# Output row pairs on partitions 0 to 99 for one quad of batches and on 28 to 127 for the next

## The chip, the cores and the metric

The kernel runs on one core of a Trainium2 chip. The metric is the device time of one execution in microseconds; before the change the median of three runs is 1459.87 us (1458.11, 1459.87 and 1463.94).

## What is computed

For 2048 batches of 200 fields with 64 features each, every field is multiplied by a 64 x 64 weight of its own, and the results are multiplied with all fields of the same batch. All values are fp32; the output is 2048 x 200 x 200, that is 327.68 MB.

```python
# r_feature: (2048, 200, 64), L0_rec_weight: (200, 64, 64)
bilinear = jnp.einsum('bie,ied->bid', feature, weight)
out = jnp.einsum('bid,bjd->bij', bilinear, feature)
```

## The kernel before

The 2048 batches are worked through in 16 blocks of 128 batches. The 200 fields of a batch form 100 pairs; the two fields of a pair lie one above the other on 128 partitions (64 features each), field 2m on the lower half and field 2m+1 on the upper. A line is 4 pairs, a group 8 pairs (`GROUPS`, 13 of them with a last one of 4), a quad 4 batches (`R = 4`, 32 quads to a block), and a set half a quad, 2 batches (`PB = 2`, 64 sets to a block, 1024 in all).

The stages of a block are these:

- SP loads a group of fields of all 128 batches into `x` (`load_x`, L152), with batches on the partitions.
- TensorE transposes it against the identity into PSUM (`transposes`, L214), and ScalarE copies the result into `xt` (`store_xt`, L292), features on the partitions.
- TensorE multiplies each field of the group by its weight (`bilinear`, L230), and ScalarE copies the result into `bl` (`store_bl`, L302).
- VectorE gathers the fields of a quad from `xt` into a window `win` (L345, L352, L353). In blocks of even number ScalarE also gathers the quad's weighed fields from `bl` into `rows` (`fill_rows`, L312); in odd blocks they lie one behind another in `bl` already.
- TensorE makes the scores of a set (`scores`, L248): for each of its 2 batches and each of the two fields of a pair one product, with the 100 weighed fields as the stationary operand (64 partitions x 100 columns) and the 200 fields of the window moving. The result is 100 partitions (row pairs) x 800 elements in one of `TILES = 3` tiles of PSUM, `ps`.
- The staging copy (`stage`, L278) takes that tile to one of `OSLOTS = 10` slots of `staging`: ScalarE for even sets, VectorE for odd ones. It waits until the slot's last stores have landed (`out_written`, `rest_written`).
- SP stores row pairs 0 to 95 of each set (`store`, L164, 300 KB), and POOL row pairs 96 to 99 of two sets at a time (`store_rest`, L196, 25 KB). SP's queue holds the loads of `x` too, in program order.

The order of the work is written out by hand. The scores of block n are interleaved with the transposes and the bilinear products of block n + 1: the tables `transposed_at` and `weighed_at` say after which set which group of the next block follows. These sets have even numbers, so a run of scores between two other pieces mostly holds the second set of one quad and the first set of the next. `xt` and `bl` are single: what block n has read is written over by block n + 1, and for this reason their two axes (lines and quads) change places from block to block.

In the trace one fp32 product of the program stands as two matmul records, each with a weight load (PEld) before it; the transposes stand as one.

Of the kernel before, what the change touches and what calls it, by code (L numbers as in the profile page):

```python
# [9 lines left out]
def feature_interaction(nc, feature, weight, out):  # L10
# [33 lines left out]
    FA = FH // 16 * 16  # L44
    assert 2 * E == 128 and B % NB == 0 and FH % 8 == C and R == 2 * PB
    assert PB * F <= 512 and OSLOTS % 2 == 0
# [15 lines left out]
    with ctx:  # L62
# [14 lines left out]
        rows = sbuf("rows", [128, RSLOTS, R, FH])  # L77
        staging = sbuf("staging", [FH, OSLOTS, PB, 2, F])
# [6 lines left out]
        ident_zero = sem("ident_zero")  # L85
        ident_ready = sem("ident_ready")
# [25 lines left out]
        def line_of_xt(n, t):  # L112
            return xt[:, t, :, :, :] if n % 2 == 0 else xt[:, :, t, :, :]

        def group_of_xt(n, u):
            lines = slice(2 * u, 2 * u + GROUPS[u] // C)
            if n % 2 == 0:
                return xt[:, lines].rearrange("p l k c r -> p k l (c r)")
            return xt[:, :, lines].rearrange("p k l c r -> p k l (c r)")

        def quad_of_xt(n, k):
            return xt[:, 0:LINES, k, :, :] if n % 2 == 0 else xt[:, k, 0:LINES, :, :]

        def group_of_bl(n, u):
            if n % 2 == 0:
                return bl[:, 8 * u:8 * u + GROUPS[u], :]
            return bl[:, :, 8 * u:8 * u + GROUPS[u]]

        def quad_of_bl(n, k):
            assert n % 2 == 0  # L130
            return bl[:, 0:FH, R * k:R * (k + 1)].rearrange("p m r -> p r m")
# [14 lines left out]
        def _(sp):  # L146
# [38 lines left out]
        def _(pool):  # L185
# [6 lines left out]
            def store_rest(s):  # L192
                slot = s % OSLOTS
                wait_staged(pool, s - 1)
                wait_staged(pool, s)
                nc.gpsimd.dma_start(out_v[FA:FH, PB * (s - 1):PB * (s + 1), :],  # L196
                                    staging[FA:FH, slot - 1:slot + 1].rearrange("p s b h j -> p (s b) (h j)")
                                    ).then_inc(rest_written[slot // 2], 16)
# [5 lines left out]
        def _(pe):  # L204
# [31 lines left out]
            def scores(n, k, i):  # L236
                s = n * SETS_B + 2 * k + i
                if k == 0 and i == 0:
                    pe.wait_ge(bl_stored, (n + 1) * NG)
                if i == 0:  # L240
                    pe.wait_ge(win_filled, n * QUADS + k + 1)
                    if n % 2 == 0:
                        pe.wait_ge(rows_filled, n // 2 * QUADS + k + 1)
                if s >= TILES:
                    wait_staged(pe, s - TILES)
                for b in range(PB):
                    for h in range(2):
                        last = nc.tensor.matmul(ps[s % TILES][0:FH, h, F * b:F * (b + 1)],  # L248
                                                row_of_bl(n, R * k + PB * i + b)[64 * h:64 * h + 64],
# [21 lines left out]
        def stage(engine, copy, staged, s):  # L271
# [11 lines left out]
        def _(act):  # L283
# [20 lines left out]
            def fill_rows(n, k):  # L304
# [7 lines left out]
                nc.scalar.copy(rows[:, q % RSLOTS], quad_of_bl(n, k)).then_inc(rows_filled, 1)  # L312
# [25 lines left out]
        def _(dve):  # L338
# [16 lines left out]

            LAST = BLOCKS * QUADS
# [28 lines left out]
```

## Time and profile before

| | |
|---|---|
| median of three runs | 1459.87 us (1458.11 to 1463.94) |
| profiled execution, its span | 1464.8 us |
| TensorE matmul / weight load busy | 95% / 80% |
| VectorE / ScalarE busy | 80% / 70% |
| queue of SP and ACT (q1), share of the 16 DMA engines | 89.2% |
| queue of POOL (q0), share of the 16 DMA engines | 6.9% |
| HBM read / written | 108.13 MB / 327.68 MB |
| chain that ended last: scores, bilinear, transposes on PE | 29% + 24% + 6% of the span |

For the profiled execution its span is the only time there is; it is 4.9 us (0.3%) above the median of the runs. Times in the rows further down are microseconds from the start of the span, unless marked ns. An engine's busy time says how long instructions of it were running; the chain that ended last follows the work back from the last instruction, at each step to what released it, and so tells which engine was waited for. A "waits" row tells for how long an engine stood idle before an instruction and what ended that.

### The profile page before, as it was taken

To read this page: it belongs to the slowest core of one execution; us is meant where nothing else is said; L and a number is where in the kernel's file an instruction comes from. 1 tells how busy PE (TensorE), PEld (TensorE's weight loads), DVE (VectorE), ACT (ScalarE), POOL (GpSimd) and SP (SyncE) were. 2 spreads that over 40 slices of the span, in tenths; PEclk is the share of its full clock that TensorE was granted. 3 is DMA by queue.
4 is the path that set the end of the run, shared out by engine and by line. 5 is a ranking of instruction groups with operands and counts; after the bars stand their busy time and mean duration, and the time that the engine had idled before them with its cause. 6 is when DMAs were issued, how large, how long until landed. Compare 5 with 4: busy or idle time off the path is not lost.

```text
span 1464.8 us, 40299 instructions
## 1 busy us (share of the span) xinstructions
PE 1388.5 (95%) x16192; PEld 1173.2 (80%) x16192; DVE 1167.6 (80%) x2048; ACT 1021.0 (70%) x1185; POOL 293.9 (20%) x518
## 2 busy tenths in 40 slices
PE   7999999999999999899999999999999999999965
PEld 6788887878878788788888888888888888878754
DVE  0478888788787888778888888887878788787897
ACT  4788567876688665886668866688567885678732
POOL 0012212122221212112122122221222222121222
PEclk9999999999999999999999999999999999999999
DMA  9799999999999999999999999999999999999898
GB/s 228 215 305 292 295 315 309 316 301 307 303 295 310 293 306 308 299 320 304 307 313 308 312 299 316 312 297 326 296 320 301 314 309 295 308 303 324 263 276 258
DMA packets 280920, 438.60 MB, mean 299 GB/s; under 512 B 53408, under 2 KB 252064, under 8 KB 280736
## 3 DMA queue, kind: packets, MB, share of 16 engines
q1 hardware_dynamic: 256160, 422.79, 89.2%
q0 software_dynamic: 24576, 13.24, 6.9%
q8 instruction: 130, 2.13, 0.6%
q14 instruction: 54, 0.44, 0.1%
HBM read 108.13 MB, written 327.68 MB: 298 GB/s over the span
## 4 chain that ended last, share of the span: by engine, by line
PE 59%; DVE 13%; issue 10%; ACT 10%; DMA 6%; SPq 2%; POOLq 0%; ACTq 0%; DVEq 0%
PE ps L248 29%; PE made L230 23%; DVE staging L278 7%; ACT xt L292 6%; PE made L214 6%; DMA out_dram<-staging 5%; DVE win L345 4%; ACT rows L312 2%; DVE win L352 2%; ACT staging L278 1%; PE ps L230 1%; DMA x<-feature_dram 1%; SPq L164 1%; SPq L152 1%; DVE win L353 1%
## 5 line engine op out<-in xcount | busy, mean ns | idle before, releaser
L278 DVE COPY staging<-ps 100x800 f32<-100x800 f32 x512 | 503.6, 984 | 202.0 <-PE ps L248 197.9
L278 ACT COPY staging<-ps 100x800 f32<-100x800 f32 x512 | 423.6, 827 | 267.0 <-PE ps L248 252.6
L196 POOL DMA_DIRECT2D out_dram<-staging x512 | 293.2, 573 | 1162.9 <-ACT staging L278 790.8
L248 PE MATMUL ps<-win,bl 64*100 64x200 f32 x4096 | 409.5, 338 | 32.3 <-DVE staging L278 32.2
L248 PE MATMUL ps<-win,rows 64*100 64x200 f32 x4096 | 412.3, 340 | 12.6 <-DVE staging L278 9.7
L248 PEld LDWEIGHTS ps<-win,bl 64*100 64x100 f32 x4096 | 326.8, 162 | 84.3 <-DVE win L353 35.8
L230 PE MATMUL made<-xt,w 64*64 64x128 f32 x6000 | 369.9, 272 | 11.1 <-ACT xt L292 5.0
L230 PEld LDWEIGHTS made<-xt,w 64*64 64x64 f32 x6000 | 322.7, 133 | 69.0 <-ACT xt L292 43.6
L248 PEld LDWEIGHTS ps<-win,rows 64*100 64x100 f32 x4096 | 328.3, 163 | 61.8 <-issue 36.2
L345 DVE COPY win<-xt 128x400 f32<-128x400 f32 x512 | 276.2, 540 | 64.1 <-ACT xt L292 48.3
L302 ACT COPY bl<-made 128x1024 f32<-128x1024 f32 (+1 forms) x195 | 191.0, 980 | 126.6 <-PE made L230 126.3
L312 ACT COPY rows<-bl 128x400 f32<-128x400 f32 x256 | 231.6, 905 | 0.0
L214 PE MATMUL made<-ident,x 128*128 128x128 f32 x1552 | 214.6, 281 | 8.9 <-DMA x<-feature_dram 8.1
L353 DVE COPY win<-win 64x400 f32<-64x400 f32 x512 | 214.6, 419 | 6.7
L292 ACT COPY xt<-made 128x1024 f32<-128x1024 f32 (+1 forms) x202 | 198.9, 985 | 25.0 <-PE made L214 25.0
L214 PEld LDWEIGHTS made<-ident,x 128*128 128x128 f32 x1552 | 166.6, 141 | 61.2 <-issue 59.8
L352 DVE COPY win<-win 64x400 f32<-64x400 f32 x512 | 187.3, 366 | 16.0
L230 PE MATMUL ps<-xt,w 64*64 64x128 f32 x400 | 25.8, 281 | 0.0
L230 PEld LDWEIGHTS ps<-xt,w 64*64 64x64 f32 x400 | 22.9, 139 | 2.2 <-issue 2.2
L302 ACT COPY bl<-ps 128x1024 f32<-128x1024 f32 (+1 forms) x13 | 12.6, 981 | 12.1 <-PE ps L230 12.1
L214 PE MATMUL ps<-ident,x 128*128 128x128 f32 x48 | 7.4, 304 | 1.9 <-DMA x<-feature_dram 1.9
L214 PEld LDWEIGHTS ps<-ident,x 128*128 128x128 f32 x48 | 5.8, 154 | 3.3 <-DMA x<-feature_dram 3.0
(8 smaller groups left out, 8.2 us busy)
## 6 DMA issues: line engine op xcount, KB each, us to landing
out_dram<-staging SPq DMA_DIRECT2D x1024, 300.0 KB, 6.0
x<-feature_dram SPq DMA_DIRECT2D x192, 512.0 KB, 6.5
out_dram<-staging POOLq DMA_DIRECT2D x512, 25.0 KB, 5.3
x<-feature_dram SPq DMA_DIRECT2D x16, 256.0 KB, 5.5
w<-weight_dram SPq DMA_DIRECT2D x24, 128.0 KB, 6.5
w<-weight_dram SPq DMA_DIRECT2D x2, 64.0 KB, 5.4
```

The lines of the kernel that those rows point to most:

```text
L152: sp.dma_start(x[:, at % XSLOTS, 0:size], feature_v[n * NB:(n + 1) * NB, 16 * E * u:16 * E * u + size]).then_inc(x_loaded[at % XSLOTS], 16)
L196: nc.gpsimd.dma_start(out_v[FA:FH, PB * (s - 1):PB * (s + 1), :], staging[FA:FH, slot - 1:slot + 1].rearrange("p s b h j -> p (s b) (h j)" ...
L214: last = nc.tensor.transpose(transpose_tile(n, u)[:, c // C, :, c % C, :], x[:, at % XSLOTS, 2 * E * c:2 * E * (c + 1)], ident[:])
L230: last = nc.tensor.matmul(bilinear_tile(n, u)[64 * h:64 * h + 64, c // 4, NB * (c % 4):NB * (c % 4 + 1)], w[64 * h:64 * h + 64, m, :], lin ...
L248: last = nc.tensor.matmul(ps[s % TILES][0:FH, h, F * b:F * (b + 1)], row_of_bl(n, R * k + PB * i + b)[64 * h:64 * h + 64], win[64 * h:64 * ...
L278: copy(staging[:, slot, :, :, :].rearrange("p b h j -> p h b j"), ps[s % TILES][0:FH, :, 0:PB * F].rearrange("p h (b j) -> p h b j", j=F)) ...
L292: nc.scalar.copy(group_of_xt(n, u), transpose_tile(n, u).rearrange("p l k c r -> p k l (c r)")).then_inc(xt_stored, 1)
L302: nc.scalar.copy(group_of_bl(n, u), weighed.rearrange(cells, b=NB)).then_inc(bl_stored, 1)
L312: nc.scalar.copy(rows[:, q % RSLOTS], quad_of_bl(n, k)).then_inc(rows_filled, 1)
L345: nc.vector.tensor_copy(win[:, q % WSLOTS, :, 1:F + 1:2].rearrange("p r (g c) -> p r g c", c=C), quad_of_xt(n, k).rearrange("p g c r -> p ...
L352: nc.vector.tensor_copy(win[64:128, slot, :, 0:F:2], win[0:64, slot, :, 1:F + 1:2])
L353: nc.vector.tensor_copy(win[0:64, slot, :, 2:F + 1:2], win[64:128, slot, :, 1:F + 1:2]).then_inc(win_filled, 1)
```

## The change

Of two successive quads one keeps its 100 row pairs on partitions 0 to 99, the other has them on partitions 28 to 127 (`first_partition`, `LOW = 28`). To get them there, the stationary operand of the scores of such a quad is read from 28 elements further ahead, so that it has 128 columns of which the first 28 are a margin; the staging copy then takes 128 partitions. The margin is zero where nothing else was written to it: VectorE sets the heads of `rows` and one corner of `bl` once, and TensorE waits for it (`margin_zero`) at the start of each block. For the margin to lie ahead of the data, the lines of `xt` and the fields in `bl` begin at line 7 and element 28 of the 32 lines and 128 elements (`LINE0 = 7`), where they began at 0. So that places come free in the same order as before, the quads of a block are worked through from the eighth on, and around (`place`). SP's store of such a quad takes partitions 32 to 127 (row pairs 4 to 99) where the other takes 0 to 95, and POOL's takes partitions 28 to 31 where the other takes 96 to 99.

```diff
+    LOW = NB - FH
+    LINE0 = LOW // C
...
-        rows = sbuf("rows", [128, RSLOTS, R, FH])
-        staging = sbuf("staging", [FH, OSLOTS, PB, 2, F])
+        rows = sbuf("rows", [128, RSLOTS, R, NB])
+        staging = sbuf("staging", [NB, OSLOTS, PB, 2, F])
...
+        def place(k):
+            return (k + LINE0) % QUADS
...
+        def first_partition(s):
+            return LOW if s // 2 % 2 else 0
...
-        def row_of_bl(n, b):
+        def row_of_bl(n, k, r, low):
             if n % 2:
-                return bl[:, b, 0:FH]
-            return rows[:, (n // 2 * QUADS + b // R) % RSLOTS, b % R, :]
+                return bl[:, R * place(k) + r, LOW - low:NB]
+            return rows[:, (n // 2 * QUADS + k) % RSLOTS, r, LOW - low:NB]
...
-                sp.dma_start(out_v[0:FA, PB * s:PB * (s + 1), :], staging[0:FA, slot]
+                low, b = first_partition(s), batch(s)
+                first = FH - FA if low else 0
+                sp.dma_start(out_v[first:first + FA, b:b + PB, :], staging[low + first:low + first + FA, slot]
                              ).then_inc(out_written[slot], 16)
...
                 if k == 0 and i == 0:
                     pe.wait_ge(bl_stored, (n + 1) * NG)
+                    pe.wait_ge(margin_zero, 2)
...
+                low = first_partition(s)
                 for b in range(PB):
                     for h in range(2):
-                        last = nc.tensor.matmul(ps[s % TILES][0:FH, h, F * b:F * (b + 1)],
-                                                row_of_bl(n, R * k + PB * i + b)[64 * h:64 * h + 64],
+                        last = nc.tensor.matmul(ps[s % TILES][0:low + FH, h, F * b:F * (b + 1)],
+                                                row_of_bl(n, k, PB * i + b, low)[64 * h:64 * h + 64],
...
-            copy(staging[:, slot, :, :, :].rearrange("p b h j -> p h b j"),
-                 ps[s % TILES][0:FH, :, 0:PB * F].rearrange("p h (b j) -> p h b j", j=F)
+            top = first_partition(s) + FH
+            copy(staging[0:top, slot, :, :, :].rearrange("p b h j -> p h b j"),
+                 ps[s % TILES][0:top, :, 0:PB * F].rearrange("p h (b j) -> p h b j", j=F)
                  ).then_inc(staged, 1)
...
-                nc.scalar.copy(rows[:, q % RSLOTS], quad_of_bl(n, k)).then_inc(rows_filled, 1)
+                nc.scalar.copy(rows[:, q % RSLOTS, :, LOW:NB], quad_of_bl(n, k)).then_inc(rows_filled, 1)
...
+            nc.vector.memset(rows[:, :, :, 0:LOW], 0.0).then_inc(margin_zero, 1)
+            nc.vector.memset(bl[:, 0:LOW, 0:LOW], 0.0).then_inc(margin_zero, 1)
```

On TensorE the runs of scores keep their places, and each is divided by width. Here is the order on TensorE early in block 1 before the change, where L214 are transposes, L230 bilinear products and L248 scores; behind an operation stand its output and inputs, output partitions x elements, and how many such products follow each other:

```order
L214 MATMUL made<-ident,x 128x32x4 x8
L248 MATMUL ps<-win,bl 100x200 x8
L230 MATMUL made<-xt,w 64x128 x16
L248 MATMUL ps<-win,bl 100x200 x8
L214 MATMUL made<-ident,x 128x32x4 x8
```

And the same place with the change, where the lines are L237, L253 and L273:

```order
L237 MATMUL made<-ident,x 128x32x4 x8
L273 MATMUL ps<-win,bl 128x200 x4
L273 MATMUL ps<-win,bl 100x200 x4
L253 MATMUL made<-xt,w 64x128 x16
L273 MATMUL ps<-win,bl 100x200 x4
L273 MATMUL ps<-win,bl 128x200 x4
L237 MATMUL made<-ident,x 128x32x4 x8
```

Each run of eight products has become four of one width and four of the other, and of two runs one begins with 128 output partitions. In the whole order 194 runs of scores that follow transposes or bilinear products begin with 128, and 196 with 100.

On VectorE the program begins like this before the change (L345, L352 and L353 fill the window):

```order
L345 COPY win<-xt 128x4x100 x2
L352 COPY win<-win 64x4x100
L353 COPY win<-win 64x4x100
L345 COPY win<-xt 128x4x100
L352 COPY win<-win 64x4x100
```

With the change (L371, L378 and L379 fill the window):

```order
L382 MEMSET rows 128x12x28
L383 MEMSET bl 128x28x28
L371 COPY win<-xt 128x4x100 x2
L378 COPY win<-win 64x4x100
L379 COPY win<-win 64x4x100
```

The two memsets stand ahead of the first copy into the window; behind them the order on VectorE is the one of before.

## Rows read from the trace of the kernel before

**Rows 1.** The page: span, and busy time of each engine with its share and instructions.

```profile
span 1464.8 us, 40299 instructions
...
PE 1388.5 (95%) x16192; PEld 1173.2 (80%) x16192; DVE 1167.6 (80%) x2048; ACT 1021.0 (70%) x1185; POOL 293.9 (20%) x518
```

**Rows 2.** Busy times by stretch, two blocks: columns are in the first row.

```profile
core 0: us, PE busy (x) PEld busy (x) DVE busy (x) ACT busy (x) POOL busy (x), PEclk, DMA share, GB/s
...
151.45:327.90 176.45, 172.41 (x2027) 145.87 (x2026) 146.12 (x257) 127.52 (x148) 36.76 (x65) 1.00 0.98 308
```

**Rows 3.** Chain of waits, whole span: start us, us, what; one mark a block.

```profile
151.45 2.96 PE ps L248 x32
...
327.90 2.96 PE ps L248 x32
...
684.93 2.96 PE ps L248 x32
...
1214.23 2.96 PE ps L248 x32
```

**Rows 4.** Waits, whole span: us in total, times, longest us.

```profile
DVE win L345 <- ACT xt L292: 48.3, 1, 48.3
...
ACT staging L278 <- DMA out_dram<-staging: 6.6, 4, 2.3
```

**Rows 5.** Chain of waits in block 7, from 690 us on.

```profile
690.46 1.90 PE made L230 x32
692.36 1.53 PE ps L248 x16
693.89 1.02 PE made L214 x8
```

**Rows 6.** Chain of waits in block 6, one round and the next one's start.

```profile
606.53 1.02 ACT xt L292
607.60 1.96 PE made L230 x32
609.56 1.56 PE ps L248 x16
...
612.65 1.03 ACT xt L292
```

**Rows 7.** Chain of waits in the last block: VectorE's copy 20 quads apart, its last piece.

```profile
1400.46 0.97 DVE staging L278
...
1446.34 0.97 DVE staging L278
...
1455.36 1.00 DVE staging L278
```

**Rows 8.** SP's stores (L164): us from issue to landing.

```profile
DMA to landing us min/median/max: 2.6/6.0/8.4
```

**Rows 9.** Timeline of TensorE and its weight loads in block 7: start us, us, what.

```profile
706.81 1.60 PE L248 MATMUL ps<-win,bl 64*100 64x200 f32 x16
...
708.08 0.33 PE L248 MATMUL ps<-win,bl 64*100 64x200 f32 x2
708.34 0.20 PEld L230 LDWEIGHTS made<-xt,w 64*64 64x64 f32 x4 [0.26 <-issue]
```

**Rows 10.** Groups by shape in two short stretches, first passes of bursts: busy us, mean ns.

```profile
L248 PE MATMUL ps<-win,bl 64*100 64x200 f32 x2 | 0.4, 410 | 0.0
...
L230 PE MATMUL made<-xt,w 64*64 64x128 f32 x2 | 0.3, 320 | 0.0
```

**Rows 11.** Groups by shape, whole span: busy us, mean ns, idle before, releasers.

```profile
L278 ACT COPY staging<-ps 100x800 f32<-100x800 f32 x512 | 423.6, 827 | 267.0 <-PE ps L248 252.6 <-DMA out_dram<-staging 6.6 <-issue 5.9
...
L248 PEld LDWEIGHTS ps<-win,rows 64*100 64x100 f32 x4096 | 328.3, 163 | 61.8 <-issue 36.2 <-ACT staging L278 16.6 <-DVE win L353 5.0
...
L230 PEld LDWEIGHTS made<-xt,w 64*64 64x64 f32 x6000 | 322.7, 133 | 69.0 <-ACT xt L292 43.6 <-issue 25.4
...
L292 ACT COPY xt<-made 128x1024 f32<-128x1024 f32 x186 | 189.3, 1018 | 25.0 <-PE made L214 25.0
```

More of the change, by code:

```diff
@@ L44, in feature_interaction @@
     FA = FH // 16 * 16
+    LOW = NB - FH
+    LINE0 = LOW // C
     assert 2 * E == 128 and B % NB == 0 and FH % 8 == C and R == 2 * PB
-    assert PB * F <= 512 and OSLOTS % 2 == 0
+    assert PB * F <= 512 and OSLOTS % 2 == 0 and LOW % C == 0 and LOW % R == 0
     feature_v = feature.rearrange("b f e -> b (f e)")
@@ L85, in feature_interaction @@
         ident_zero = sem("ident_zero")
+        margin_zero = sem("margin_zero")
         ident_ready = sem("ident_ready")
@@ L112, in line_of_xt @@
         def line_of_xt(n, t):
-            return xt[:, t, :, :, :] if n % 2 == 0 else xt[:, :, t, :, :]
+            return xt[:, LINE0 + t, :, :, :] if n % 2 == 0 else xt[:, :, LINE0 + t, :, :]
         def group_of_xt(n, u):
-            lines = slice(2 * u, 2 * u + GROUPS[u] // C)
+            lines = slice(LINE0 + 2 * u, LINE0 + 2 * u + GROUPS[u] // C)
             if n % 2 == 0:
@@ L119, in group_of_xt, with batch @@
             return xt[:, :, lines].rearrange("p k l c r -> p k l (c r)")
+        def place(k):
+            return (k + LINE0) % QUADS
         def quad_of_xt(n, k):
-            return xt[:, 0:LINES, k, :, :] if n % 2 == 0 else xt[:, k, 0:LINES, :, :]
+            lines = slice(LINE0, LINE0 + LINES)
+            return xt[:, lines, place(k), :, :] if n % 2 == 0 else xt[:, place(k), lines, :, :]
+        def first_partition(s):
+            return LOW if s // 2 % 2 else 0
         def group_of_bl(n, u):
             if n % 2 == 0:
-                return bl[:, 8 * u:8 * u + GROUPS[u], :]
-            return bl[:, :, 8 * u:8 * u + GROUPS[u]]
+                return bl[:, LOW + 8 * u:LOW + 8 * u + GROUPS[u], :]
+            return bl[:, :, LOW + 8 * u:LOW + 8 * u + GROUPS[u]]
         def quad_of_bl(n, k):
             assert n % 2 == 0
-            return bl[:, 0:FH, R * k:R * (k + 1)].rearrange("p m r -> p r m")
-        def row_of_bl(n, b):
+            return bl[:, LOW:NB, R * place(k):R * (place(k) + 1)].rearrange("p m r -> p r m")
+        def row_of_bl(n, k, r, low):
             if n % 2:
-                return bl[:, b, 0:FH]
-            return rows[:, (n // 2 * QUADS + b // R) % RSLOTS, b % R, :]
+                return bl[:, R * place(k) + r, LOW - low:NB]
+            return rows[:, (n // 2 * QUADS + k) % RSLOTS, r, LOW - low:NB]
+        def batch(s):
+            n, k, i = s // SETS_B, s % SETS_B // 2, s % 2
+            return n * NB + R * place(k) + PB * i
         def wait_staged(engine, s):
@@ L195, in store_rest @@
                 wait_staged(pool, s)
-                nc.gpsimd.dma_start(out_v[FA:FH, PB * (s - 1):PB * (s + 1), :],
-                                    staging[FA:FH, slot - 1:slot + 1].rearrange("p s b h j -> p (s b) (h j)")
+                low, b = first_partition(s), batch(s - 1)
+                first = 0 if low else FA
+                ms = slice(first, first + FH - FA)
+                ps_ = slice(low + first, low + first + FH - FA)
+                nc.gpsimd.dma_start(out_v[ms, b:b + 2 * PB, :],
+                                    staging[ps_, slot - 1:slot + 1].rearrange("p s b h j -> p (s b) (h j)")
                                     ).then_inc(rest_written[slot // 2], 16)
```

## The prediction

> **What bounds the kernel now.** I read the totals of the engines first, then the blocks, then the chain of waits, and the transfers last, because two resources look full at once. TensorE is busy 95% of the span [rows 1], and over two whole blocks of batches the transfers take 98% of the 16 DMA engines' time [rows 2]. A change to where the stores read from could therefore matter much, or not at all. What decides it is which of the two the others wait for.
>
> The marks in the chain of waits give the pitch of the blocks: the same place of blocks 1, 3, 7 and 13 stands at 151.45, 327.90, 684.93 and 1214.23 us [rows 3]. The first step is two blocks, 176.45 us, and the last is six, 529.30, that is 176.43 for every two. So even a pace is no picture of a queue that overflows. The step between, from block 3 to block 7, is four blocks and takes 357.03 us where 2 x 176.45 = 352.90 is due: **4.1 us** were lost there, and in that stretch the chain of waits names stores. In all of the trace ScalarE's staging copy waited 4 times for a store, 6.6 us together; VectorE's never did for long enough to be listed [rows 4].
>
> Inside a block with an odd number the chain is TensorE alone: bursts of bilinear products (1.90), scores (1.53) and transposes (1.02) follow each other without a gap [rows 5]. In a block with an even number it goes round ScalarE: copy of the transposed tile 1.02 to 1.03, bilinear burst 1.96, one score burst 1.56, and back, 6.12 us a round (612.65 less 606.53) [rows 6]. In the last block, where nothing is interleaved, it is VectorE: 20 of its quads take 1446.34 - 1400.46 = 45.88 us, 2.29 each [rows 7], and it is also VectorE for some six quads around each border of two blocks.
>
> So transfers cost little now: the 4.1 us in the middle, and part of the end. The last staging copy starts at 1455.36 and takes 1.00, the span ends at 1464.8 [rows 1, 7]: 8.4 us in which nothing but stores goes on. The fastest store landed 2.6 us after its issue, so at most 8.4 - 2.6 = **5.8 us** of the end is queueing [rows 8].
>
> **The change, part by part.**
>
> *Weight loads of 128 columns.* Half of the quads now have 128 columns in the stationary operand where all had 100. A fp32 product stands in the trace as two passes, and passes go in pairs, one for each half of the partitions. In the middle of a burst the load is hidden: 16 score passes take 1.60 us, the first pair 0.41 of it, so the other seven pairs come every (1.60 - 0.41) / 7 = 170 ns [rows 9, 10]. A load of 100 columns lasts 163 ns, one of 64 lasts 133 [rows 11], 0.83 ns a column, so one of 128 would last 163 + 28 x 0.83 = 186 ns, longer than the pitch. But bilinear bursts of 32 take 1.96 us, the first pair 0.32 of it [rows 6, 10], so their pairs come every (1.96 - 0.32) / 15 = 109 ns although their loads last 133: the last 24 ns of a load do not hold back the next pass. 186 - 24 = 162 is still under 170, so I take nothing here. The bounds are 0 and 186 - 162 = 24 ns a pair, the latter if the whole recorded load counts.
>
> *The first load of a burst* is exposed. The first passes of a score burst take 410 ns, the last two 0.33 us [rows 9, 10]: 80 ns more for 100 columns, the same 0.8 ns a column as above, so 128 columns add some 23 ns. Bursts straddle quads, as the order on TensorE shows: half of them now begin with a quad of 128 columns, 13 in a block (12 in the 15th, none in the 16th). On the path are all 13 in the seven odd blocks, and in the eight even ones the 6 that follow bilinear products: (7 x 13 + 8 x 6) x 23 ns = **+3.2 us**. Bounds: 0, and all 194 of them, 4.5 us.
>
> *Staging copies over 128 partitions.* ScalarE's copy of 800 elements on 100 partitions takes 827 ns, 1.03 ns an element; its copy of 1024 on 128 partitions takes 1018, 0.99 an element [rows 11]. More partitions cost nothing. 0.
>
> *ScalarE's copy into rows* now writes four runs of 100 with gaps. No row shows that step alone. The staging copy writes runs of 200 and costs at most 4% more an element (1.03 to 0.99) than the one beside it; 4% of 400 elements at 1.03 ns is 16 ns, in 256 copies at most 4 us. I take 0, as ScalarE's fixed start is in the 4% too.
>
> *Two memsets on VectorE* (336 and 784 elements a partition). Nothing of that kind stands on this engine; a copy of 800 elements takes 1.00 us [rows 7], so 1.4 us as a bound. VectorE idles 48.3 us before its first copy [rows 4], so they are hidden, unless that wait shrinks to under 1.4 us. TensorE's new wait on them, once a block, is satisfied before the first score; 0.
>
> *Order of the batches, 28 places on.* Same instructions, same number and size of stores on SP and POOL, each queue in the same place; 0.
>
> *Where the stores read.* SP's stores read 96 partitions from 0, then 96 from 32; POOL's small ones 96 to 99, then 28 to 31. All that shows a price is the landing, 2.6 us from the issue at best and 6.0 in the median [rows 8]. Something holds the stores up, but whether it is the partitions they read, the memory they write, or the loads beside them, no row tells. The SBUF page of the Trainium skill (Door 1: The DMA port swizzle) states that partitions 0 to 63 lie on one set of eight ports and 64 to 127 on the other eight, so a store of 0 to 95 puts two thirds of its bytes on eight ports, and the alternation evens that out; no row here shows ports. From its 27.2 GB/s a port I estimate 307,200 x 2/3 / (8 x 27.2) = 0.94 us for the crowded half of a store. One store comes every 1.38 us (176.45 us for 128 of them [rows 2]). By that page even the crowded side keeps up, so it would not change the sum; by the rows all that easier stores can give back is the 4.1 and the 5.8. I take half of the first and a third of the second, -2 and -2, since the cause of the queue is open. Bounds: 0 and **-9.9 us**.
>
> Sum, against the profiled span: 1464.8 + 3.2 - 2 - 2 = 1464.0. The median of the three runs, 1459.87, lies 4.9 under that span, so I predict 1464.0 - 4.9 = **1459.1 us**: no change. A measurement of this kernel tells some 0.5%, 7.3 us, from no change.
>
> **The rivals.**
>
> *Stores flow freely (chance 0.20).* Both losses go: +3.2 - 9.9 = -6.7 us, 1453.2. For it: stores take more than twice their best time to land. Against it: the chain names them in one stretch only. From the fastest run of before (1458.11) the same gain ends at 1451.4, so four fifths of this case are faster by over 0.5%.
>
> *The whole weight load counts (0.10).* If a pass waits for the recorded end of its load, each pair of a 128-column set gets 24 ns longer. TensorE or the ring through it sets the pace in 26 quads of a block, 13 of them wide: 26 sets x 4 pairs x 24 ns = 2.5 us in each of seven odd blocks, half of that in eight even ones, where one burst of two is on the chain: 17.5 + 10 = 27.5 us, 1487. It decides from a load of 170 ns on. For it: 186 is over 170. Against it: the bilinear bursts, which run 24 ns faster than their loads last.
>
> *A change of width empties TensorE (0.05).* Wherever the kind of burst changes, the next weight load begins 0.26 us after the last pass started (708.34 against 708.08), or a little less [rows 9]. The same at every change from 100 to 128 columns would cost 0.26 + 0.10 (the exposed load, 80 + 23 ns) - 0.17 = 0.19 us; with 25 of them in each of seven odd blocks and 13 in eight even ones, 279 x 0.19 = 53 us, 1512. The page TensorEngine Tiling (Array Packing) of the Trainium skill (Tiling Modes, Key Properties) states that a switch of tiling mode drains the engine; 100 and 128 columns both need more than its 64-column tiles, so by that rule this is no switch. Every kind of burst here has another shape, so no row shows width alone.
>
> *Nothing gets easier (0.05).* The stores wait as before, and the exposed loads cost 3.2 to 4.5 us: 1459.87 + 4 = 1463.9.
>
> **How the numbers follow.** The forecast has 0.60. Faster by over 0.5% (under 1452.6): 0.16, four fifths of the first rival. Slower by over 0.5% (over 1467.2): 0.10 + 0.05 = 0.15. The rest, 0.69, is within. The range reaches down to 1451.4, the first rival from the fastest run, and up to 1468, the exposed loads with a dearer copy into rows and the scatter of the runs (1463.94 + 4); it leaves the two slow rivals out.
>
> **What would show it.** Right: odd blocks stay at one TensorE chain with bursts beginning 23 ns later every second time; two blocks take 176.7 to 177.0 us; score passes stay at some 330 ns; stores land earlier in the median; the end after the last copy is shorter. Wrong: score passes of wide sets 24 ns longer on the average (second rival), a gap inside score bursts (third), VectorE's quads in the last block longer than 2.29, or waits for stores in more than one stretch. A time under 1451 would mean that the transfers held back more than the chain of waits shows.

## The result and the profile after

The change takes **1512.03 us** (median of four runs, 1509.45 to 1516.30); the kernel before took 1459.63 beside it. The ratio is 1.0352, with a 95% interval of 1.0339 to 1.0366. The forecast was 1459.1 within 1451.4 to 1468.0: it was wrong by 53 us, and on the side that had the chance of 0.15.

The page of the changed kernel begins with span, busy times and, further down, the DMA queues (packets, MB, share of the 16 engines) and the chain that ended last:

```profile
span 1514.4 us, 40310 instructions
...
PE 1401.2 (93%) x16192; PEld 1185.4 (78%) x16192; DVE 1170.6 (77%) x2050; ACT 1015.9 (67%) x1185; POOL 293.9 (19%) x518
...
q1 hardware_dynamic: 256160, 422.79, 86.8%
q0 software_dynamic: 24576, 13.24, 7.9%
...
PE 54%; DMA 24%; ACT 8%; issue 6%; SPq 5%; DVE 2%; POOLq 0%; ACTq 0%; DVEq 0%
PE ps L273 28%; DMA out_dram<-staging 23%; PE made L253 19%; PE made L237 6%; ACT xt L318 4%; SPq L183 4%; DMA x<-feature_dram 2%; ACT rows L338 2%; DVE staging L304 1%; ACT staging L304 1%; SPq L169 1%; PE ps L253 1%; DVE win L371 0%; ACT bl L328 0%; PE ps L237 0%
```

No engine works much longer than in [rows 1]: TensorE is busy 12.7 us more, over a span that is 49.6 us longer. What is new is in the chain: 23% of the span is now the landing of stores, where it was 5%. SP's large stores (L183) show who pays:

```profile
L183 SPq DMA_DIRECT2D out_dram<-staging x1024: 317/1062/3407, 58.0 to 1509.2; - x171
...
  ACT staging L304: 110.3, 69
  DVE staging L304: 2.9, 1
...
DMA to landing us min/median/max: 2.7/6.1/9.7
```

The two rows in the middle are who waited for a store, us and times. ScalarE's staging copy stood 110.3 us in 69 waits where it stood 6.6 us in 4 [rows 4]. The landing itself has hardly moved (median 6.1 after 6.0 [rows 8]), but SP issues its stores later: on the average of the second to the fifteenth block 5.6 us behind their copies, where it was 2.6 before (from the traces' records). Issuing one takes somewhat longer, 1.06 us in the median and up to 3.41. Here is the same row before the change, and then that of e6 below, which has no small stores (ns, min/median/max):

```profile
L164 SPq DMA_DIRECT2D out_dram<-staging x1024: 317/936/3113, 56.5 to 1459.8; - x171
```

```profile
L183 SPq DMA_DIRECT2D out_dram<-staging x1024: 317/318/1629, 55.4 to 1447.9; - x171
```

POOL's small stores (L219) have no waiter. The chain of waits (start us, us, what) has such landings from the end of the second block (229.80 us) to the end, among them these:

```profile
229.80 4.53 DMA out_dram<-staging
...
690.20 4.75 DMA out_dram<-staging
...
1496.05 6.48 DMA out_dram<-staging
...
1502.62 1.00 DVE staging L304
```

Its last row is the last staging copy: from its end to that of the span pass 1514.4 - 1503.6 = 10.8 us, where it was 8.4. So the transfers, which cost 4.1 us in the middle before, now hold up the work from there to the end. Yet they do not move more. This is the busy row over the two blocks' stretch of [rows 2]:

```profile
151.45:327.90 176.45, 170.45 (x1984) 144.61 (x1982) 142.23 (x250) 125.54 (x146) 35.65 (x63) 1.00 0.96 294
```

The DMA share is 0.96 where it was 0.98, and the rate 294 GB/s where it was 308. In stores of the same number and size, 4.5% less goes through in this stretch. The lost time is waiting for stores, not more work.

### The profile page after: what moved, and what is told of

Read it like the earlier page. It is cut to its first block, busy times and chain, and to the rows that moved or that the text cites. A ratio compares the mean times of both kernels' runs of the same rounds, so it can differ in the third digit from the quotient of the medians.

```text
span 1514.4 us, 40310 instructions
## 1 busy us (share of the span) xinstructions
PE 1401.2 (93%) x16192; PEld 1185.4 (78%) x16192; DVE 1170.6 (77%) x2050; ACT 1015.9 (67%) x1185; POOL 293.9 (19%) x518
## 3 DMA queue, kind: packets, MB, share of 16 engines
q0 software_dynamic: 24576, 13.24, 7.9%
## 4 chain that ended last, share of the span: by engine, by line
PE 54%; DMA 24%; ACT 8%; issue 6%; SPq 5%; DVE 2%; POOLq 0%; ACTq 0%; DVEq 0%
PE ps L273 28%; DMA out_dram<-staging 23%; PE made L253 19%; PE made L237 6%; ACT xt L318 4%; SPq L183 4%; DMA x<-feature_dram 2%; ACT rows L338 2%; DVE staging L304 1%; ACT staging L304 1%; SPq L169 1%; PE ps L253 1%; DVE win L371 0%; ACT bl L328 0%; PE ps L237 0%
## 5 line engine op out<-in xcount | busy, mean ns | idle before, releaser
L304 DVE COPY staging<-ps 100x800 f32<-100x800 f32 (+1 forms) x512 | 504.0, 984 | 245.8 <-PE ps L273 210.2
L304 ACT COPY staging<-ps 100x800 f32<-100x800 f32 (+1 forms) x512 | 423.7, 828 | 342.3 <-PE ps L273 190.2
L219 POOL DMA_DIRECT2D out_dram<-staging x512 | 293.2, 573 | 1210.2 <-ACT staging L304 909.2
L273 PE MATMUL ps<-win,bl 64*100 64x200 f32 (+1 forms) x4096 | 417.6, 341 | 44.2 <-DVE staging L304 43.9
L273 PE MATMUL ps<-win,rows 64*100 64x200 f32 (+1 forms) x4096 | 416.7, 342 | 25.1 <-DVE staging L304 19.5
L273 PEld LDWEIGHTS ps<-win,bl 64*100 64x100 f32 (+1 forms) x4096 | 334.3, 175 | 99.2 <-issue 52.0
L273 PEld LDWEIGHTS ps<-win,rows 64*100 64x100 f32 (+1 forms) x4096 | 333.7, 175 | 76.3 <-issue 48.6
L253 PE MATMUL made<-xt,w 64*64 64x128 f32 x6000 | 369.9, 272 | 11.7 <-ACT xt L318 6.0
L253 PEld LDWEIGHTS made<-xt,w 64*64 64x64 f32 x6000 | 322.7, 133 | 67.1 <-ACT xt L318 43.4
L371 DVE COPY win<-xt 128x400 f32<-128x400 f32 x512 | 275.5, 538 | 63.5 <-ACT xt L318 47.8
L237 PE MATMUL made<-ident,x 128*128 128x128 f32 x1552 | 214.3, 280 | 15.2 <-DMA x<-feature_dram 9.3
L379 DVE COPY win<-win 64x400 f32<-64x400 f32 x512 | 214.9, 420 | 6.7
L237 PEld LDWEIGHTS made<-ident,x 128*128 128x128 f32 x1552 | 166.6, 141 | 65.4 <-issue 63.3
L378 DVE COPY win<-win 64x400 f32<-64x400 f32 x512 | 187.4, 366 | 16.0
L253 PE MATMUL ps<-xt,w 64*64 64x128 f32 x400 | 25.3, 278 | 0.0
L253 PEld LDWEIGHTS ps<-xt,w 64*64 64x64 f32 x400 | 22.4, 137 | 2.2 <-issue 2.2
L237 PE MATMUL ps<-ident,x 128*128 128x128 f32 x48 | 7.4, 304 | 2.7 <-DMA x<-feature_dram 2.7
L237 PEld LDWEIGHTS ps<-ident,x 128*128 128x128 f32 x48 | 5.9, 154 | 4.2 <-DMA x<-feature_dram 4.0
```

Source lines behind the costliest of these rows:

```text
L219: nc.gpsimd.dma_start(out_v[ms, b:b + 2 * PB, :], staging[ps_, slot - 1:slot + 1].rearrange("p s b h j -> p (s b) (h j)")).then_inc(rest_w ...
L237: last = nc.tensor.transpose(transpose_tile(n, u)[:, c // C, :, c % C, :], x[:, at % XSLOTS, 2 * E * c:2 * E * (c + 1)], ident[:])
L253: last = nc.tensor.matmul(bilinear_tile(n, u)[64 * h:64 * h + 64, c // 4, NB * (c % 4):NB * (c % 4 + 1)], w[64 * h:64 * h + 64, m, :], lin ...
L273: last = nc.tensor.matmul(ps[s % TILES][0:low + FH, h, F * b:F * (b + 1)], row_of_bl(n, k, PB * i + b, low)[64 * h:64 * h + 64], win[64 * ...
L304: copy(staging[0:top, slot, :, :, :].rearrange("p b h j -> p h b j"), ps[s % TILES][0:top, :, 0:PB * F].rearrange("p h (b j) -> p h b j", j=F)
L371: nc.vector.tensor_copy(win[:, q % WSLOTS, :, 1:F + 1:2].rearrange("p r (g c) -> p r g c", c=C), quad_of_xt(n, k).rearrange("p g c r -> p ...
```

## The experiments

All edits are made to the changed kernel. "Low" is partitions 0 to 99 for a set, "high" is 28 to 127. The kernel before took 1460 to 1462 us beside each of them. First a table of all, by what the stores read; the intervals stand with the runs below.

| run | SP's large stores read | POOL's small stores read | us |
|---|---|---|---|
| the change | 0–95, 32–127 by turns | 96–99, 28–31 by turns | 1512.0 |
| e1 | 0–95 | 96–99 | 1460.4 |
| e2 | 32–127 | 28–31 | 1467.6 |
| e3 | 0–95 | 96–99 (products and copies alternate) | 1463.4 |
| e4 | by turns | 96–99 | 1628.5 |
| e5 | 0–95 | by turns | 1577.9 |
| e6 | by turns | none | 1454.9 |
| e12 | 0–95 | none | 1451.3 |
| e7 | 32–127 | 96–99 | 1780.9 |
| e9 | 0–95 | 64–67 | 1461.5 |
| e10 | 0–95 | 32–35 | 1778.5 |
| e8 | by turns of four quads | by turns of four quads | 1518.5 to 1578.6 |
| e11 | 4–99, 28–123 by turns | 0–3, 124–127 by turns | 1539.5 |
| e13 | 4–99 | 0–3 | 1463.6 |
| e14 | 28–123 | 124–127 | 1467.3 |
| e15 | by turns | by turns, four sets later | 1599.9 |
| e16 | by turns of a block | by turns of a block | 1464.0 |
| e17 | by turns, each fifth twice | none | 1519.2 |
| e18 | 0–95, each fifth twice | none | 1533.0 |

### Is it one side, or the computing? (e1, e2, e3)

```diff
         def first_partition(s):
-            return LOW if s // 2 % 2 else 0
+            return 0         # e1; e2: return LOW
```

> The changed kernel with every quad on partitions 0 to 99; the rotated order of batches, the shifted places in xt and bl, the wider rows and staging and the memsets stay. Three theories of the 52 us: (A) stores from alternating partitions get in each other's way; (B) the far side is slow by itself (stores from 32 to 127, small stores from 28 to 31); (C) it is not the partitions of the stores at all but what came with them: order of batches in memory, shifted places, wide products and copies. A and B expect the time of before, 1460 within 6 us, and hardly a wait for stores. C expects some 1512 if the order of batches or the places do it, and 1460 if the wide products or copies do.

> The changed kernel with every quad on partitions 28 to 127: all products 128 columns wide, all stores of SP from 32 to 127, all of POOL from 28 to 31. (A) expects the time of before plus the exposed weight loads, 1460 to 1467, because nothing alternates. (B) expects about twice the loss, 1550 to 1570. (C) with wide products expects about twice the loss too, 1550 to 1570, but with waits of TensorE and not of stores.

In e3 products and copies alternate as in the change, but both stores read the places of a low set:

```diff
-staging[low + first:low + first + FA, slot]
+staging[0:FA, slot]
...
-                ps_ = slice(low + first, low + first + FH - FA)
+                ps_ = slice(FA, FH)
```

> The changed kernel, products and copies alternating as they do there, but every store of SP reads partitions 0 to 95 of staging and every one of POOL 96 to 99, so that the values stored for every second quad are other rows of the tile. Same stores in number, size and target. (A) and (B) expect 1460 to 1467 (the exposed loads remain). (C) expects 1512.

Measured, in this order: 1460.37 us (ratio to before 1.0001, 95% interval 0.9990 to 1.0012; so in brackets from here on), 1467.62 (1.0050, 1.0035 to 1.0065) and 1463.39 (1.0015, 1.0006 to 1.0024). Everything that the change adds to the engines costs 2 us, or 3 by the difference of the two runs, and writing the output rows in another order costs nothing, as e3 does both. The other 49 us (1512.03 less 1463.39) hang on the partitions that the stores read.

### Which of the two stores? (e4, e5, e6, e12)

e4 leaves SP's alternation and has POOL read 96 to 99 always; e5 has SP read 0 to 95 always and leaves POOL's alternation; e6 is the change without POOL's stores and without the waits for them; e12 is e6 with all quads low.

```diff
-                ps_ = slice(low + first, low + first + FH - FA)
+                ps_ = slice(FA, FH)                                    # e4
...
-staging[low + first:low + first + FA, slot]
+staging[0:FA, slot]                                                    # e5
...
-            for s in range(1, BLOCKS * SETS_B, 2):
-                store_rest(s)                                          # e6, e12
...
-            return LOW if s // 2 % 2 else 0
+            return 0                                                   # e12
```

> The changed kernel, but POOL's small stores always read partitions 96 to 99; SP's stores alternate as in the change. Four rows of every second quad get other values. If the large stores do it (A, or B by 32 to 127), some 1512 as with the change. If the small ones from 28 to 31 do it (B's other half), 1460 to 1467.

> The changed kernel, but SP's large stores always read partitions 0 to 95, and only POOL's small stores alternate (96 to 99, then 28 to 31, which lies inside the range that the large stores read). Half of the rows stored get other values. Theories after the first four runs: (A1) the large stores lose time whenever they change sides; (A2) the large ones are as quick as ever, and what gets slow are POOL's small ones, whenever their partitions lie in the range of the large stores in flight; each small packet then blocks its DMA engine. A1 expects 1463 within 4 us. A2 expects a slow run, 1500 or more.

> The changed kernel without POOL's small stores and without the waits for them: row pairs 96 to 99 or 0 to 3 are never written. The large stores alternate as in the change. A1 expects 1490 to 1510, the loss of the change nearly whole, less the 7% of DMA time that the small stores take. A2 expects 1463 or less, the time of before plus the exposed weight loads at most, and no waits for stores.

> All quads on 0 to 99 as in e1, without POOL's small stores and without the waits for them (row pairs 96 to 99 are never written): the counterpart of e6, where the large stores alternate. If alternating sides eases the large stores, they land later here than e6's 4.8 us in the median, by the 0.5 us or more that a crowded side would cost; if it does nothing, 4.8 again. The time is 1452 to 1456 either way, as e6's 1454.86 holds the exposed weight loads of 2 to 3 us.

Measured: e4 1628.49 (1.1147, 1.1130 to 1.1164), e5 1577.88 (1.0806, 1.0779 to 1.0832), e6 1454.86 (0.9959, 0.9944 to 0.9974), e12 1451.28 (0.9939, 0.9925 to 0.9954). Half an alternation is worse than the whole, and without the small stores there is no loss: e6 is 3.6 us above e12, which is the price of the wider products again. The transfers of e6, by kind (KB each, median us to landing), and then of e12:

```profile
out_dram<-staging SPq DMA_DIRECT2D x1024, 300.0 KB, 4.8
```

```profile
out_dram<-staging SPq DMA_DIRECT2D x1024, 300.0 KB, 4.7
```

The small stores, 3% of the bytes, make the large ones land a good microsecond later (5.9 in e1), and the alternation of the large ones alone neither shortens nor lengthens their landing.

### Which partitions are bad for a small store? (e7, e9, e10)

e7 puts all quads high with POOL reading 96 to 99. e9 and e10 put all quads low, and POOL reads 4 partitions within the range of SP's stores:

```diff
-            return LOW if s // 2 % 2 else 0
+            return 0                                   # e9, e10; e7: return LOW
...
-                ps_ = slice(low + first, low + first + FH - FA)
+                ps_ = slice(64, 64 + FH - FA)          # e9; e10: from 32; e7: slice(FA, FH)
```

> All quads on partitions 28 to 127 as in the run e2, large stores always from 32 to 127, but POOL's small stores read 96 to 99, inside that range, where e2 had them on 28 to 31. Four rows of every quad get other values. A1 expects e2's time, 1467 within 5 us. A2 expects the slowest run of all, 1630 or more, since in e4 this held for every second quad only.

> All quads on partitions 0 to 99 and large stores from 0 to 95, as in e1, but POOL's small stores read partitions 64 to 67, inside the range of the large ones. Four rows of every quad get other values. Two readings of what makes a small store slow: (R) its partitions lie in the range that the large stores in flight read; (P) partitions share ports by the page's table, and what counts is how many rows the two kinds of stores read through one port: here 64 to 67 share one with 96 to 99, of which the large stores read 4, so 8 with the small ones, no more than in the kernel before. R expects a time as in e7, 1700 or more. P expects the time of before, 1460 within 5 us.

> As e9, but the small stores read partitions 32 to 35, which by the page share a port with 0 to 3; the large stores read all 8 of these, so 12 rows go through one port. Four rows of every quad get other values. R and P both expect a time as in e7, 1700 or more. If this is quick and e9 too, then neither holds, and it is 28 to 31 or 96 to 99 against large stores that begin at 32 that matters.

Measured: e7 1780.88 (1.2183, 1.2152 to 1.2214), e9 1461.51 (1.0004, 0.9991 to 1.0016), e10 1778.54 (1.2181, 1.2162 to 1.2199). The two last differ by one number, 64 or 32. The longest wait of e10 that ends with a store (us, times, longest), of which e9 has none:

```profile
ACT staging L304 <- DMA out_dram<-staging: 317.9, 160, 4.5
```

POOL's queue on the page, of e10 and then of e9:

```profile
q0 software_dynamic: 24576, 13.24, 9.9%
```

```profile
q0 software_dynamic: 24576, 13.24, 6.5%
```

And the busy rows of both, from 400 to 800 us, where DMA share and GB/s are the last two numbers:

```profile
400.00:800.00 400.00, 332.40 (x3716) 271.01 (x3718) 269.53 (x469) 233.74 (x278) 66.97 (x117) 0.98 0.88 251
```

```profile
400.00:800.00 400.00, 389.84 (x4575) 329.66 (x4576) 332.79 (x584) 293.63 (x343) 83.53 (x146) 1.00 0.98 307
```

The packets of the same 13.24 MB take almost twice as long (9.9% of 1778 us are 176 us of each engine, 6.5% of 1461 are 95), and the whole goes at 251 GB/s in place of 307, while the DMA engines have 12% of their time free. That a small store reads within SP's range is harmless (e9); which four partitions it reads decides over 317 us.

The Trainium skill (SBUF — State Buffer, Door 1: The DMA port swizzle) has a table of which eight partitions share a port: 32 to 35 share theirs with 0 to 3, and 64 to 67 with 96 to 99. By that table SP's stores read eight rows of the small store's port in e10 and e7, and four in e1, e2, e9, e13 and e14; in e4 and e5 it is eight in half of the quads. These times agree with the grouping: eight gives 1779 to 1781 us, half of the quads 1578 to 1628, four 1460 to 1468. The change itself and e11, in which both kinds of store change side, do not follow from it; they come next.

### What does the alternation do, then? (e8, e11, e13 to e16)

In each quad of the change itself the small store reads the same place beside the large one as in e1 or e2. But SP issues its stores 4 to 6 us behind their copies there (from the trace's records, averages of the blocks from the second on), some two quads, and POOL 0.7 us. Two quads behind is the same side again. But a large store lands 6 us after its issue, so some four of them are under way at a time, two of each side, and a small store from 96 to 99 goes out beside large ones from 32 to 127 as well, as in e7: by the records half of the large stores under way beside a small one are of the other side. The idea tested first was that this is the cause. A rarer change of side should then cost less (e8, e16), and dealing the rows the other way, with small stores at the outer edges, should cost nothing (e11; e13 and e14 are its two sides alone). A later small store was meant to go along with its own side (e15).

```diff
-            return LOW if s // 2 % 2 else 0
+            return LOW if s // 8 % 2 else 0            # e8; e16: s // SETS_B % 2
...
-                first = FH - FA if low else 0
+                first = 0 if low else FH - FA          # SP's store: e11, e13, e14
...
-                first = 0 if low else FA
+                first = FA if low else 0               # POOL's: e11, e13, e14
...
-                wait_staged(pool, s)
+                wait_staged(pool, min(s + 4, BLOCKS * SETS_B - 1))     # e15
```

> The changed kernel with sides that change every four quads in place of every quad; everything computed. A quarter of the changes of side remain. Both A1 and A2 expect a quarter of the loss, 1463 + 12 = 1475 within 6 us, since with A2 the small stores meet large ones of the other side at a change only. A time as with the change (1512) would say that it is the two sides as such, and a time of 1463 that only quads in flight together matter and four quads hide it.

> The change with the rows dealt out the other way round, everything computed: for a quad on 0 to 99 SP stores partitions 4 to 99 and POOL 0 to 3, for one on 28 to 127 SP stores 28 to 123 and POOL 124 to 127. The small stores never read a partition that any large store reads, and by the table of ports never one of the crowded ones. R and P expect 1455 to 1463: no waits for stores but the exposed weight loads. If the alternation itself were at fault it would be 1490 or more again.

Both missed. e8 took 1518.54 us in one run and 1558.00 to 1578.55 in three more: a quarter of the changes of side did not cost a quarter of the loss. That it costs more than the change (1509.45 to 1516.30) is not shown, as one run lies only 2 us above. Nor did the quarter follow from the idea: by the records of e8 0.38 of the large stores under way beside a small one are of the other side, where it is 0.50 in the change. e11 took 1539.50 (1.0553, 1.0524 to 1.0583). By the table of ports its small stores meet four rows in large stores of either side, as in e1, and by the grouping it would be at 1460 to 1468. In e11 POOL's packets are quick, quicker than in e9, and the staging copies wait all the same. Its row of POOL's queue, its wait, and its busy row:

```profile
q0 software_dynamic: 24576, 13.24, 5.1%
```

```profile
ACT staging L304 <- DMA out_dram<-staging: 120.7, 78, 4.9
```

```profile
400.00:800.00 400.00, 371.00 (x4264) 311.73 (x4261) 311.94 (x545) 265.44 (x314) 78.07 (x137) 1.00 0.94 290
```

> The outer dealing of rows of the run that took 1539.5 us (SP's stores 4 to 99, POOL's 0 to 3), but every quad on partitions 0 to 99: no alternation. If the dealing itself costs (theory C): 1515 to 1550. If what costs is that the side changes (theories A and B): 1458 to 1463, as with all quads low and the other dealing (1460.4).

> The same dealing with every quad on partitions 28 to 127 (SP's stores 28 to 123, POOL's 124 to 127). Dealing itself costs (C): 1515 to 1560. The change of side costs (A, B): 1463 to 1469, as with all quads high and the other dealing (1467.6).

> The change, with POOL's small store waiting for the copy four sets later (5.5 us), about as far behind its copies as SP's large stores are in the change (5 to 6 us). Theory A (a small store that runs ahead meets large stores of the other side, which read many rows from its port): the small one now goes together with large ones of its own side, 1457 to 1470. Theory B (it is the change of side under two queues, whatever the ports): stays at 1505 to 1520. Rival: slots come free later by the delay, and staging copies wait more: above 1520.

> The change, with the side changing once a block (every 32 quads) in place of every quad: 15 changes in the run. Theory A: collisions only for some 6 us at each change, 1462 to 1470 (between all low 1460.4 and all high 1467.6). Theory B, at some 0.8 us for each change of side as with a change every four quads (1567.9 less 1464, over 127): 1472 to 1480. If two sides as such cost, however seldom they change: 1500 or more.

Measured: e13 1463.60 (1.0016, 1.0006 to 1.0026), e14 1467.30 (1.0033, 1.0017 to 1.0049), e16 1463.96 (1.0018, 1.0009 to 1.0027). Neither dealing of the rows costs by itself, and neither do two sides in one kernel, if they change once a block. It is the frequent change of side. The records of e16, second to fifteenth block, show what happens at its few changes: the 18 small stores beside which over 0.3 of the large ones were of the other side landed in 5.9 us in the median, the 388 beside which none was in 5.3. In the same blocks of e5 the small stores from 28 to 31, which meet eight rows, landed in 5.9 and those from 96 to 99, which meet four, in 5.4. So within one run a small store is slower beside large ones that read eight rows of its port. From run to run the landing does not tell it: it is 5.1 in e10, where all meet eight, and 5.5 both in the change and in e11, where none does. The row of e16 that answers to the one of e11:

```profile
400.00:800.00 400.00, 388.60 (x4546) 330.90 (x4542) 330.25 (x579) 291.96 (x341) 82.55 (x145) 1.00 0.97 303
```

e15 took 1599.89 (1.0920, 1.0872 to 1.0967), which was the rival of its expectation: the wait moved to the slots. In its profiled run (1615.59 us, the longest of four) nobody waits for SP's stores; for POOL's (L219) it is:

```profile
who waited for it (us, times):
  ACT staging L304: 368.9, 265
  DVE staging L304: 27.8, 48
```

The small stores now hold the slots too long. And the delay did not part the sides: half of the large stores under way beside a small one are of the other side here too (0.50). So this run does not tell whether meeting the other side is the cause.

### Is it the large stores' own rate? (e17, e18)

The runs without small stores move 3% fewer bytes, and a lower rate of the alternating stores could have been hidden by that. So SP's queue was loaded alone until it set the pace: every fifth large store is issued a second time, into spare memory, with alternation (e17, from e6) and all low (e18, from e12). `here` is what the store before it reads.

```diff
+                if stores_of(slot) > 1:
+                    sp.dma_start(spare[s // 5].rearrange("b p e -> p b e"), here.rearrange("p b h j -> p b (h j)")).then_inc(out_written[slot], 16)
```

> The alternation of the large stores without POOL's small ones, and every fifth large store issued twice, the second time to spare memory: SP's store bytes are 20% more (15% more than both queues of the change), so that transfers set the pace. Theory E (the alternation lowers the rate at which the large stores can go, which is hidden while 4% of the bytes are left out): 3 to 8% above its twin with all quads low. Theory F (it needs the small stores on POOL's queue): within 0.5% of the twin, but for the 3 us of wider products. Time itself between 1480 and 1700, as no run shows the rate at saturation.

> The twin of the run with loaded alternating stores: all quads on partitions 0 to 99, no small stores, every fifth large store issued twice, the second time to spare memory. Between 1470 and 1650. Theory E: 3 to 8% under the alternating one. Theory F: the two within 0.5%.

Measured: e17 1519.22 (1.0397, 1.0371 to 1.0423) and e18 1532.97 (1.0485, 1.0443 to 1.0527). The alternating one is 0.9% *faster*, though it has the dearer products; its longest run, 1522.36, is under the shortest of the other, 1526.00. The stretch of e17, then of e18, each from the profiled run, which is the shortest of e17 (1513.64) and the longest of e18 (1540.76):

```profile
400.00:800.00 400.00, 376.51 (x4351) 317.32 (x4348) 312.81 (x561) 275.15 (x324) 0.00 (x0) 1.00 1.00 331
```

```profile
400.00:800.00 400.00, 368.36 (x4252) 306.07 (x4250) 303.18 (x541) 263.34 (x311) 0.00 (x0) 1.00 0.99 321
```

So the alternation raises what the large stores reach when the queue is full: by 0.9% in the time, and by 3% in this stretch of these two runs (331 to 321 GB/s). It does not lower it. And e17 moves 488 MB in almost the time in which the change moves 439: with the alternation, 13 MB of small stores cost as much as 63 MB of second large ones.

## Why the prediction was wrong

**What bounds the kernel** was read rightly but used on one side only. The transfers stood at 0.98 of the DMA engines and cost little [rows 2, 4]. From that a bound was taken for easier stores, -9.9 us, and none for harder ones. The same rows say that a loss of rate of a few per cent has hardly any slack to go into.

**The step that failed is "Where the stores read"**, with its bounds of 0 and -9.9 us. Its words "whether it is the partitions they read, the memory they write, or the loads beside them, no row tells" were right, and from them followed a bound upward too, which was not set. The term was +49 us (1512.0 less e3's 1463.4), where -4 was taken. What the prediction worked out from the Trainium skill (SBUF — State Buffer, Door 1: The DMA port swizzle) looked at the large stores alone and at ports on the average. For them it points the right way: without small stores the alternation gains 0.9% of the time when the queue is full (e17, e18), and nothing when it is not, as large stores from 0 to 95 then land in 4.7 us already (e12). What it left out is the small store, whose place beside the large ones can cost 22% (e7, e10). The prediction named the partitions of POOL's stores; the sum had no term for them.

**The rest of the sum** held. A weight load of 128 columns takes 186 ns as worked out, and passes do not wait for it. Groups by shape (busy us, mean ns, idle before and its releasers):

```profile
L338 ACT COPY rows<-bl 128x400 f32<-128x400 f32 x256 | 232.2, 907 | 0.0
...
L273 PE MATMUL ps<-win,bl 64*128 64x200 f32 x2048 | 226.5, 344 | 21.4 <-DVE staging L304 21.3
...
L273 PE MATMUL ps<-win,bl 64*100 64x200 f32 x2048 | 221.7, 339 | 22.8 <-DVE staging L304 22.6 <-ACT staging L304 0.2
...
L304 ACT COPY staging<-ps 128x800 f32<-128x800 f32 x256 | 211.9, 828 | 180.6 <-PE ps L273 100.0 <-DMA out_dram<-staging 51.9 <-issue 27.6
...
L273 PEld LDWEIGHTS ps<-win,bl 64*128 64x128 f32 x2048 | 172.6, 186 | 50.5 <-issue 25.6 <-DVE win L379 16.9 <-ACT staging L304 6.9
...
L383 DVE MEMSET bl<- 128x784 f32 x1 | 0.7, 712 | 0.1
...
L382 DVE MEMSET rows<- 128x336 f32 x1 | 0.3, 338 | 0.9 <-PEq L403 0.9
```

The 5 ns between the mean passes (344 and 339) come from the first ones of bursts: without passes of over 380 ns, the records have 328 and 329 ns. Two bursts of block 7 and the passes around them (min, median and max in the middle, forms last) show 433 for the longest, 410 + 23 as predicted [rows 10], and 329 for the median:

```profile
L273 PE MATMUL ps<-win,bl x34: 327/329/433, 720.8 to 726.8; 64*100 64x200 f32 x18, 64*128 64x200 f32 x16
```

The exposed loads were to cost 3.2 us. e3 and e16, which have them, stand 2.1 and 2.7 us above before, and e6 stands 3.6 above its twin e12, which has none. This fits, but is near what the runs can tell: e13, without wide products, is 2.3 above before too. The staging copy over 128 partitions takes 828 ns, as over 100 [rows 11]. The memsets take 1.05 us together, within the bound of 1.4, and nothing waits for them. The order of the batches costs nothing (e1 is before again, to 0.01%).

**The rivals.** None foresaw it. Stores do not flow freely; they flow less, and so they do not wait as before either. (The first rival's chance was misread too: its own figure, 1453.2, is not under 1452.6, so it does not follow that four fifths of it are faster by over 0.5%.) The whole weight load does not count. The third, "a change of width empties TensorE", has the time that came, 1512, and is nevertheless false. It would have made a burst with both widths 0.19 us longer. The first of those two bursts has eight passes of each width, by shape within it (busy us, mean ns):

```profile
L273 PE MATMUL ps<-win,bl 64*100 64x200 f32 x8 | 0.9, 349 | 0.0
L273 PE MATMUL ps<-win,bl 64*128 64x200 f32 x8 | 0.8, 328 | 0.0
```

and on the timeline of TensorE (start us, us) it lasts 1.60, as the burst of one width does in [rows 9], and the other, which begins wide, 1.63:

```profile
722.09 1.60 PE L273 MATMUL ps<-win,bl 64*100 64x200 f32 x16
723.62 1.96 PE L253 MATMUL made<-xt,w 64*64 64x128 f32 x32
725.52 1.63 PE L273 MATMUL ps<-win,bl 64*128 64x200 f32 x16
```

A total that agrees says nothing for a mechanism: e3 has all the changes of width and takes 1463.4.

The signs that the prediction named were good ones: the trace shows "waits for stores in more than one stretch" (69 of them for 4), while passes, bursts and copies are as forecast.

**What is shown, and what stays open.** Shown is that the loss needs both the frequent change of side and POOL's small stores (e6, e16, e17 against the change), and that small stores from some partitions cost 8 to 22% without a change of side of the large ones (e5, e7, e10). Not settled is how the two act on each other in the change. Small stores that meet large ones of the other side would fit the change and e16, but not e11, where by the table no small store meets eight rows of its port. Nor does this give the size: in the change and in e4 the same half of the large stores under way beside a small one read eight rows of its port, and e4 loses 165 us beside e3 where the change loses 49. In e7, e10 and e11 the DMA engines together are less busy (0.90, 0.88 and 0.94 of the same stretch), although stores wait to be taken, as if some of the 16 were late while others idle. The records of the transfers don't name the engine, so this is a guess.

No version that stores the whole output beats the kernel before. e1, which is that kernel with the change's order and places, equals it, and e12's 8.9 us are the most that could be had from the small stores, by having none.

## What to carry to other kernels

Where the transfers stand at 98% and nobody waits for them yet, give an edit that moves them a bound on the side of the loss too: a few per cent of rate are a few per cent of the time. Look at the smallest store before the largest: 4 rows on the wrong four partitions cost more here than all 96 others could gain, and one run with only that store moved (e9 against e10) tells it. And when the number of a rival comes true, test its mechanism with a run that keeps the mechanism and takes the rest away.

## What was not expected of the hardware

- Small stores of 4 partitions (25 KB, 3% of the bytes) set the rate of all transfers by the four partitions they read: 307 GB/s from 64 to 67, 251 from 32 to 35, beside the same large stores.
- A change of side every four quads is no better than one every quad (1518.5 to 1578.6 us, against 1512), and one every 32 quads costs nothing (1464). No reason was found.
- Without small stores and with a full queue, large stores that alternate between 0 to 95 and 32 to 127 are done 0.9% sooner than those from 0 to 95 alone (1519.2 to 1533.0 us; 331 and 321 GB/s in the stretch shown).
